# One listed order of steps for all eight groups, in place of a periodic plan, in the first three stages of an attention stack on one core

## What is computed

```python
x = _L0_xattn_ref(x, ctx, ...)       # stage 0, "chan": attention over the 128 channels' 256 columns, residual
x = _L1_xattn_ref(x, ctx, ...)       # stage 1: ln1, self attention (16 heads), ln2, cross attention, ln3, MLP (gelu)
x = _L2_xattn_ref(ctx, x, ...)       # stage 2, "lat": 16 heads over 256 keys with a mask, rms norm, MLP (gelu)
x = _L3_xattn_ref(x, ctx, ctx, ...)  # stage 3: two wide cross attentions and an MLP, not touched
```

```python
scores = einsum('bhqd,bhkd->bhqk', q, k) / scale      # and its mask
out = einsum('bhqk,bhkd->bhqd', softmax(scores), v)
```

## Time and profile before

| | us |
|---|---|
| median of 3 runs | 2092.16 |
| lowest and highest | 2090.68, 2093.16 |
| the profiled execution | 2091.94 |
| its span, first to last instruction | 2090.0 |

### The profile page before, as it was taken

One profiled execution on the slowest core, in us unless ns is written; L12 is line 12 of the kernel. 1 busy time (PEld: TensorE's weight loads), 2 busy tenths in 40 slices (PEclk: granted clock), 3 DMA queues, 4 the chain that ended last, 5 costly groups with the idle time before them and its releaser, 6 DMA issues.

```text
span 2090.0 us, 43191 instructions
## 1 busy us (share of the span) xinstructions
PE 1932.3 (92%) x14880; PEld 1680.3 (80%) x14880; DVE 1276.7 (61%) x4143; ACT 1184.2 (57%) x3879; POOL 678.0 (32%) x613
## 2 busy tenths in 40 slices
PE   5679899999999999888999999999899999999889
PEld 3557678787777777667999999999799999999778
DVE  4668897878787865455555555556455555555653
ACT  3377787878787876436444444443644444444631
POOL 1233444444444443523222222132322222213452
PEclk7799999999999999999999999999999999999999
DMA  7000000000000000001000000000000000000100
GB/s 264 8 9 7 7 12 2 11 4 4 4 4 4 2 2 1 22 11 36 24 25 16 25 20 15 25 16 26 19 18 26 15 25 20 15 20 0 41 11 31
DMA packets 24635, 44.35 MB, mean 21 GB/s; under 512 B 2336, under 2 KB 12064, under 8 KB 23584
## 3 DMA queue, kind: packets, MB, share of 16 engines
q1 hardware_dynamic: 24336, 42.19, 6.1%
q10 hardware_dynamic: 144, 0.20, 0.0%
HBM read 40.28 MB, written 2.10 MB: 20 GB/s over the span
## 4 chain that ended last, share of the span: by engine, by line
PE 48%; DVE 2%; ACT 2%; issue 1%; POOL 1%; ACTq 0%; DVEq 0%; POOLq 0%
PE general L1965 32%; PE o_psum L2022 6%; PE scores L2004 5%; PE pT_psum L2081 3%; PE scores L2131 1%; ACT probs L1636 1%; POOL probs L1540 1%; PE o_psum L2131 1%; PE pT_psum L2131 1%; PE general L1976 0%; DVE oT L1807 0%; ACT oT L1652 0%; DVE guess L1317 0%; DVE row_stats L1769 0%; DVE totals L1798 0%
## 5 line engine op out<-in xcount | busy, mean ns | idle before, releaser
L567 POOL TENSOR_TENSOR probs<-probs,rsums 128x512 f32<-128x512 f32 (+1 forms) x288 | 283.9, 998 | 473.6 <-DVE rsums L794 473.0
L1540 POOL TENSOR_TENSOR probs<-probs,rsums 128x512 f32<-128x512 f32 x128 | 133.4, 1042 | 733.5 <-DVE rsums L1800 733.5
L617 ACT ACTIVATE probs<-negated,negmax 128x128 f32<-128x128 f32 (+1 forms) x768 | 325.4, 430 | 12.1 <-DVE negmax L785 11.8
L1644 ACT COPY probsT<-pT_psum 128x512 f32<-128x512 f32 x128 | 75.0, 586 | 282.9 <-PE pT_psum L2081 282.9
L1112 PE MATMUL pT_psum<-ident,probs 128*128 128x128 f32 x1072 | 175.1, 285 | 53.8 <-ACT probsT L625 26.4
L1112 PEld LDWEIGHTS pT_psum<-ident,probs 128*128 128x128 f32 x1072 | 124.5, 144 | 108.0 <-issue 59.3
L1965 PE MATMUL general<-hT,w_qk 128*128 128x512 f32 x768 | 206.3, 404 | 1.8 <-ACT kT L1619 1.5
L1965 PE MATMUL general<-w_o,oT 128*128 128x256 f32 x1536 | 197.7, 282 | 1.6 <-ACT oT L1652 0.9
L1965 PEld LDWEIGHTS general<-w_o,oT 128*128 128x128 f32 x1536 | 187.7, 188 | 11.6 <-DVE oT L1807 4.0
L1965 PE MATMUL general<-ctxT,w_qk 128*128 128x512 f32 x750 | 194.1, 394 | 2.9 <-DVEq L222 2.9
L1636 ACT ACTIVATE probs<-scores,negmax 128x128 f32<-128x128 f32 x512 | 180.5, 370 | 24.0 <-DVE negmax L1792 24.0
(11 more groups left out here) (199 smaller groups left out, 3920.9 us busy)
## 6 DMA issues: line engine op xcount, KB each, us to landing
raw_qk<-w_qk_dram SPq DMA_DIRECT2D x32, 256.0 KB, 2.9
weights_a<-weights_a_dram SPq DMA_DIRECT2D x2, 2048.0 KB, 18.0
raw_v<-w_v_dram SPq DMA_DIRECT2D x16, 256.0 KB, 2.7
raw_vrows<-vrows_dram SPq DMA_DIRECT2D x16, 256.0 KB, 3.4
raw_o<-w_o_dram SPq DMA_DIRECT2D x16, 256.0 KB, 2.7
weights_a<-weights_a_dram SPq DMA_DIRECT2D x3, 1024.0 KB, 11.3
ctx_in<-ctx_dram SPq DMA_DIRECT2D x8, 256.0 KB, 2.8
X<-x_dram SPq DMA_DIRECT2D x8, 256.0 KB, 16.1
```

The lines of the kernel that those rows point to most:

```text
L567: nc.gpsimd.tensor_tensor(pr, pr, rsums[:, n % 4, 0:segs].unsqueeze(2).broadcast_to([P, segs, width(kind) // segs]), ALU.mult).then_inc(s[ ...
L617: last = nc.scalar.activation(probs[:, n % PROBS, i * wide:(i + 1) * wide], src[:, i * wide:(i + 1) * wide], ACT.Exp, scale=1.0 if kind == ...
L1540: nc.gpsimd.tensor_tensor(pr, pr, rsums[:, t % 2, :].unsqueeze(2).broadcast_to([P, NB, P]), ALU.mult).then_inc(s["probs_ready"], 1)
```

## The change

The plan with its due times goes. Each engine's order is written out for all eight groups. A stream (the blocks of units, the work, the norms, the adds, the loads) is a list of its own, and a string with one letter for each step says from which stream the engine takes its next step. For TensorE the letters are s scores, t turn, v values, w work, f first; for VectorE f front, r rsum, c copy, o values read, w read, n norm; for ScalarE e exps, c copy, o values read, w read; for GpSimd p normalise, a add, x cross mask, y lat mask, l the low part of a first step; h, k and z are the first steps of the others.

No step is added, taken away or given to another engine: 734 steps on TensorE, 844 on VectorE, 691 on ScalarE, 351 on GpSimd, 19 loads. Written out, the plan's streams and the listed ones are the same: blocks, work, norms, adds and loads have no element in another place. What differs is how the streams of one engine are merged: 474 of TensorE's 734 places hold another step than before, 632 of VectorE's, 479 of ScalarE's and 327 of GpSimd's. The steps that build on them, `stages_0_to_2` with its waits, are unchanged.

```diff
-PERIOD = 100.0
...
-SCORES = {('chan', 0): -56.65, ('chan', 2): -53.05, ('self', 0): 2.04, ('self', 4): 11.35, ('cross', 0): 80.21,
-          ('cross', 4): 89.81, ('lat', 0): 224.27, ('lat', 4): 236.69, ('lat', 8): 259.02, ('lat', 12): 270.59}
...
-AFTER = {'front': {'chan': (5.08, 2.43), 'self': (1.09, 1.75), 'cross': (3.38, 1.5), 'lat': (2.64, 1.01)},
-         'exps': {'chan': (5.08, 7.01), 'self': (2.86, 3.55), 'cross': (9.41, 2.47), 'lat': (7.51, 0.99)},
...
-WORK = {'chan_v': (-94.75, 3.08), 'chan_q': (-87.99, 2.44), 'chan_k': (-73.94, 0.58), 'ln1': (-14.63, 2.21),
-        'self_q': (-13.49, 2.6), 'self_k': (-5.66, 0.18), 'self_v': (8.16, 1.36), 'cross_k': (19.72, 1.65),
...
+NORMS = ("ln1", "ln2", "ln3", "rms")
+KINDS = {"c": "chan", "s": "self", "x": "cross", "l": "lat"}
+
+
+def listed(text):
+
+    return [(name, int(g)) for name, g in (word.split("/") for word in text.split())]
+
+
+def merged(letters, **streams):
+
+
+    left = {letter: iter(steps) for letter, steps in streams.items()}
+    order = [next(left[letter]) for letter in letters]
+    assert not any(list(steps) for steps in left.values())
+    return order
+
+
+def steps_of(step, items):
+
+    return [(step, name, g, 0) for name, g in items]
...
+BLOCK_WORDS = """
+    c0 c0 s0 s0 c1 c1 x0 x0 s1 s1 c2 c2 x1 x1 s2 s2 l0 l0 c3 c3 l0 l0 x2 x2 s3 s3 l1 l1 c4 c4 l1 l1 x3 x3 s4
+    s4 l2 l2 c5 c5 l2 l2 x4 x4 s5 s5 l3 l3 c6 c6 l3 l3 x5 x5 s6 s6 l4 l4 c7 c7 l4 l4 x6 x6 s7 s7 l5 l5 l5 l5
+    x7 x7 l6 l6 l6 l6 l7 l7 l7 l7
+""".split()
+BLOCKS_A = [(KINDS[word[0]], int(word[1]), BLOCK_WORDS[:i].count(word)) for i, word in enumerate(BLOCK_WORDS)]
...
+WORK_ORDER = listed("""
+    chan_v/0 chan_q/0 chan_k/0 ln1/0 self_q/0 self_k/0 chan_v/1 self_v/0 chan_q/1 cross_k/0 chan_k/1 self_o/0
+    ln2/0 cross_q/0 ln1/1 self_q/1 self_k/1 cross_v/0 chan_v/2 self_v/1 chan_q/2 cross_k/1 chan_k/2 cross_o/0
...
+LOAD_WORDS = listed("""
+    ctx/2 ctx/3 mask_lat/1 mask_cross/2 ctx/4 mask_lat/2 mask_cross/3 ctx/5 mask_lat/3 mask_cross/4 ctx/6
+    mask_lat/4 mask_cross/5 ctx/7 mask_lat/5 mask_cross/6 mask_lat/6 mask_cross/7 mask_lat/7
+""")
...
+TENSOR_STEPS = (
+    "wwwssttvttvwwwswwswttwttvttttvwwsswtwttvtvswwswtwtwstwtvttstttvtwtwttvwtwttsvwswwwwtwttvtwvwswwwwswwtwwt"
...
+VECTOR_STEPS = (
+    "ffrffrcrroconwffffrrffrrfcfrrrcrccwnfrfffrrrcwcoonffffrwrrrffffcrffrcfrrfcrrfrcffcrfrrrcrcwcnwfnfffrrrrc"
...
+SCALAR_STEPS = (
+    "wwweeceecwwweeeeweceecewocwcoweweceecweeeeecweeweceeocwweceeceeocewwcwcooweweeewcwcwweeewweewcewweceewwc"
...
+GPSIMD_STEPS = (
+    "xppppyaxppppppppyppppaapppppxpppppppppppappppapppppaxppppppppppppppppappppppppppypapaaappppppppppxpppppp"
+    "pppppappppppppppppppyappppppaaapxpppppppppppppppppappppppppppppppaapaaypppppxpppppppppppppappppppppppppp"
+    "ppyapappppapppppxpppppapppppppppappppppppppppppaaaappppyppppppppppppppppppappappappppyppppppppppppappppp"
+    "pppaapppppppaplplalppllplalpppppppppppp")
...
+TENSOR_ORDER = merged(TENSOR_STEPS, s=[("scores", *unit) for unit in FIRST_UNITS], t=[("turn", *unit) for unit in UNITS],
+                      v=[("values", *unit) for unit in FIRST_UNITS], w=steps_of("work", WORK_ORDER),
+                      f=[("first", name, GA - 1, half) for name in FIRST_WORK for half in range(2)])
...
+GPSIMD_ORDER = merged(GPSIMD_STEPS, p=[("normalise", *unit) for unit in UNITS], a=steps_of("add", ADD_ORDER),
+                      x=[("mask", "cross", g, 0) for g in range(GA)], y=[("mask", "lat", g, 0) for g in range(GA)],
+                      l=steps_of("first_low", [(name, GA - 1) for name in FIRST_LOW]))
```

More of the change, by code:

```diff
@@ L127 @@
[L127 to L132, removed]
-LAST = PERIOD * (GA - 1)
-def by_plan(times):
-    return sorted(((name, g) for name in times for g in range(GA)), key=lambda item: times[item[0]] + PERIOD * item[1])
-BLOCKS_A = [(kind, g, first // BLOCK_UNITS[kind]) for (kind, first), g in by_plan(SCORES)]
+NORMS = ("ln1", "ln2", "ln3", "rms")
@@ new lines @@
+""")
+NORM_ORDER = listed("""
+    ln1/0 ln2/0 ln1/1 ln3/0 ln2/1 ln1/2 ln3/1 ln2/2 ln1/3 rms/0 ln3/2 ln2/3 ln1/4 rms/1 ln3/3 ln2/4 ln1/5
+    rms/2 ln3/4 ln2/5 ln1/6 rms/3 ln3/5 ln2/6 ln1/7 rms/4 ln3/6 ln2/7 rms/5 ln3/7 rms/6 rms/7
+""")
+ADD_ORDER = listed("""
+    self/0 self/1 cross/0 mlp1/0 self/2 cross/1 mlp1/1 self/3 cross/2 lat/0 mlp2/0 mlp1/2 self/4 cross/3 lat/1
+    mlp2/1 mlp1/3 self/5 cross/4 lat/2 mlp2/2 mlp1/4 self/6 cross/5 lat/3 mlp2/3 mlp1/5 self/7 cross/6 lat/4
+    mlp2/4 mlp1/6 cross/7 lat/5 mlp2/5 mlp1/7 lat/6 mlp2/6 lat/7 mlp2/7
@@ L148 @@
 USES_A = [(name[:-1] if "_down" in name else name, g) for name, g in WORK_ORDER if not name.endswith("_down1")]
-NORM_ORDER = by_plan(NORMS)
-ADD_ORDER = by_plan(ADDS)
 MASKED_UNITS = [key for key in UNITS if key[0] in ("self", "cross")]
@@ L193 @@
-VECTOR_ORDER = in_order(of_units("front", UNITS), of_units("rsum", UNITS), of_units("copy_dve", [unit for unit in UNITS if unit[2] % 2 == 1]),
-                        [step for step in of_units("values_read", FIRST_UNITS) if step[2] == "chan"],
-                        of_names("read", [item for item in WORK_ORDER if item[0] in VECTOR_READS], READ_AT), of_names("norm", NORM_ORDER, NORMS),
-                        of_last("first_high", FIRST_ROWS), of_last("first_read", FIRST_READ), of_last("first_norm", {"x": FIRST_NORM}))
@@ L197 @@
-SCALAR_ORDER = in_order(of_units("exps", UNITS), of_units("copy_act", [unit for unit in UNITS if unit[2] % 2 == 0]),
-                        [step for step in of_units("values_read", FIRST_UNITS) if step[2] != "chan"],
-                        of_names("read", [item for item in WORK_ORDER if item[0] not in VECTOR_READS and not item[0].endswith("_down0")], READ_AT),
-                        of_last("first_high", FIRST_PARTS))
-GPSIMD_ORDER = in_order(of_units("normalise", UNITS), of_names("add", ADD_ORDER, ADDS), of_names("mask", by_plan(MASKS), MASKS),
-                        of_last("first_low", FIRST_LOW))
@@ L210, in before @@
+LOAD_ORDER = [("ctx", "chan_k", g, 0) if name == "ctx" else ("mask", name.split("_")[1], g, 0) for name, g in LOAD_WORDS]
 def before(step, names, name, g, order):
```

107 lines of the change are left out of this document (63 added, 44 removed).

## The result

The changed kernel takes 2107.86 us, the median of 7 runs (2099.56 to 2109.39), against 2093.16 us before in the same session (2090.68 to 2097.7): 1.0064 times as long, with a 95% interval of 1.005 to 1.0077. I had forecast 2076 us. It is slower, by 14.7 us.

The account below looks back on a forecast made before the run. TensorE was taken to bound the middle, group 0's chain the start, a mixture the end. The terms +4.9 - 5 - 6 - 10 = -16 took 2092 to 2076 us; forecast range 2068 to 2085 (chance 0.54).

Parts of the forecast that it names:

- What bounds it: TensorE bounds the middle, where a gap costs its length; group 0's chain the first 100 us; the end is mixed.
- So no busy time is added: Same steps, engines, streams, banks and loads, so only the merging of each engine's streams changes.
- the splits of the context in the tail: GpSimd's four splits beside VectorE's fronts of group 7: 2.3 us each, at most 9.3 us on VectorE.
- signs of being wrong: A start staying 5 us late, a middle over 28 us idle, or stage 3 entered early and then waiting.
- (a): Start: GpSimd's first step waits for the cross mask's load, delaying the first products; +4.9 us, bounds 0 and +4.9.
- (b): Group 0's chain: reordered exponentials, copies and values shorten TensorE's two long gaps; -5 us, between 0 and -9.
- (c): Middle 500 us: half of TensorE's waits for copies go; -6 us, bounds +3 and -14.
- (d): Last 200 us: fewer back-to-back transposes, covered chain waits, less lower clock; -10 us, between 0 and -15.
- The rival that ended slower: Mask's load costs 4.9 us not regained, middle adds 3, end gives nothing: 2100 us, chance 0.13.
- its decision point: The slower rival decides once (b) is under 5 us and (c) and (d) together give nothing.

Follow-up runs that it names:

- a_x0: Changed kernel with GpSimd's first step, the cross mask of group 0, moved back behind the four chan products: 2102.6 us.
- psum: Pair at full work, masked scores left in their PSUM bank instead of the SBUF buffer: 2069.0 us in the listed order, 2096.9 in the plan's.
- stay: Pair with short adds and products, GpSimd waiting after each before releasing the result: 2057.6 us in the listed order, 2080.8 in the plan's.
- thin_all: Pair with four of five adds per group on 16 of 256 columns, products on 8 columns per segment: listed order 2056.1 us, plan's 2082.6.
- a_psum: Changed kernel at full work, masked scores written back to their PSUM bank instead of the SBUF buffer: 2069.0 us.
- b_psum: Kernel before (plan's order) at full work, masked scores left in their PSUM bank: 2096.9 us.
- b_thin: Kernel before (plan's order) with four of GpSimd's five adds per group on 16 of 256 columns: 2089.0 us.
- b_stay: Kernel before (plan's order) with short adds and products, GpSimd waiting after each before releasing the result: 2080.8 us.
- a_pad: Changed kernel with four of five adds per group on 16 of 256 columns, each followed by 24 GpSimd waits: 2085.4 us.
- a_thin: Changed kernel with four of GpSimd's five adds per group on 16 of 256 columns: 2091.0 us.

## Why the prediction was wrong

*What bounds it* was right and fell short: in the middle a gap of TensorE costs its length, and the long ones cost the clock as well.

*"So no busy time is added"* is the step that failed. Instructions were the same, but VectorE's maxima over masked scores took 15.5 us more, since they met GpSimd's instructions more often and for longer, and the stalls behind made TensorE's busy time grow through the clock. I had the row that shows it, an operation of 0.28 us that took 1.35 beside an add, and I priced it for one place alone, the splits of the context in the tail. The adds in the middle I didn't place against the new fronts. The Trainium skill, "SBUF — State Buffer", section "SBUF: two separate sides", says that a VectorE operation with two SBUF inputs and a GpSimd operation that reads SBUF exclude each other for a whole instruction. The traces agree for adds and products: held are the maxima over masked scores, both operands in SBUF, 78 of 109 beside GpSimd before and 89 of 112 after; of those of lat, whose scores are in PSUM, none of 140 and 132. By that rule the forecast should have had a rival with a term for every add.

The traces don't agree with it for one step: 29 of the 31 that were not held before ran beside `lat_mask`, which reads its mask from SBUF too and takes 1.07 us and more; 0.4 us was the longest of the 29. Two lines from before, GpSimd and VectorE:

```profile
363.29 1.07 POOL L561 TENSOR_SCALAR madd_lat<-mask_lat 128x256 f32<-128x256 int32 x1
```

```profile
363.77 0.28 DVE L785 CUSTOM_DVE_ANT_0 negated<-masked,madd_cross 128x128 f32<-128x128 f32 x1
```

Two of the prediction's own signs of being wrong came: a start 5 us late, and a middle with more than 28 us idle, 42.9 of the 500.

*(a), the mask's load*: +4.9 forecast, +5.3 measured (a_x0), and it stays to the end. *(b), group 0's chain*: -5 forecast, -0.7 measured. The two gaps shrank by 2.56 and 0.76 us as named, and the time went into others: in a_x0 TensorE waits 4.51 us for the second self block where it was 3.49, 1.48 us for a copy at 122.6, 1.19 us before values at 113.9. Its bounds held the value.

*(c), the middle*, is the term that carries the miss: -6 forecast, bounds -14 to +3; with the holds +27.5. Without them it is +2.2 (psum), +1.3 (stay) and -0.4 (thin_all), so within the bounds and not the gain. Of idle time the listed order has 4.7 us less in a_psum than in b_psum, near the 6, but it also does 37 matmuls more before the cut (4987 and 4950).

*(d), the tail*: -10 forecast, -15 at most. It is -19.1, and -18.9 to -21.9 without the holds. The idle time went down 9.7 us, where I had 7.6. The clock was the mis-sized term: 2 us forecast, some 7 measured, since the dips between 840 and 905 us went (windows 840 to 860 and 885 to 905: 0.74 and 0.91 before, 1.00 and 1.00 after). In the rest, where I had nothing, the changed kernel is 2.5 us longer, with a clock of 0.95 over the first 60 us behind the cut, where it was 1.00. That this is the price of the faster tail isn't shown: b_thin, b_stay and b_psum, in the plan's order, have 0.94 there, and rests of 1186.1 to 1187.5 us.

Added up without the holds, middle and tail are 19.7 us shorter in the listed order (a_psum 751.0, b_psum 770.7), against the forecast's 16. With them they are 8.4 us longer. So the hold costs the listed order 33.3 us in these stretches and the plan's 5.2 (both less what the later release of the banks costs in them). The maxima lose much in either order, 33 us before and 48 after, so it is where the holds fall that decides: before, no wait of TensorE reaches 1.3 us in the 500 us of the middle, in the changed kernel eight do, and in a_psum again none. No semaphore stands for a hold, so no list of waits shows where it will fall.

The rival that ended slower gave 2100 by the mask, no gain at the end and 3 us in the middle. Its first part was right and its decision point, nothing from (c) and (d), wasn't what happened. That the kernel came out slower, as this rival had it, was luck: the mechanism wasn't in it.

*Open*: why a_pad beats a_thin; why `lat_mask` doesn't hold; what each single add costs; and why the start of b_psum is 9.4 us longer. In that last one TensorE's idle time is nearly as before, 50.1 us for 49.4, and its busy time is 90.3 us for 81.6, at a clock of 0.74 for 0.80; b_psum's profiled execution is also 3.7 us above its median.

## What to carry to other kernels

A list of waits and semaphores is not all that ties two engines. Before an order is changed, look for operations whose duration differs with what runs on another engine, and place those first; or take away what they share, here by leaving one operand in PSUM. A term that a row of the trace shows in one place has to be counted in every place where the change lets it occur. And an order can be judged by stretches: spliced, the part that gained could be had without the part that lost.

## What the runs showed of the hardware

A held operation on VectorE lasts until the GpSimd instruction ends: 87 of the 89 in the changed kernel end 0.14 or 0.15 us behind it (0.28 us became up to 1.39 beside adds of 1.3). With one operand in PSUM the same operation was never held, in 197 that ran beside GpSimd, and takes 287 ns on the mean at 128 columns, as it does from SBUF when nothing holds it (285). Held too was an operation of the norms with one SBUF input, the variance, which takes 0.17 us alone; beside a product that ran from 231.63 on for 1.04 us:

```profile
231.74 0.97 DVE L867 TENSOR_SCALAR var<-mv 128x2 f32<-128x2 f32 x1
```

Of the eight waits of TensorE in the middle, four came with stretches at the lower of the clock's two levels: those at 266, 481, 620 and 696 us (2.49, 3.18, 3.43 and 4.50 us long) have windows of 5 us with a clock of 0.66, 0.60, 0.50 and 0.64. Around the other four (1.40, 2.54, 1.63 and 2.35 us) it stayed at 1.00, so the length of a wait alone doesn't tell. In this kernel the clock cost as much as the waits: 12 us against 11 us of idle time in the middle.
